# Attention over 128-row tiles: values zero-padded by half, grouped roots, rows added by transfers, combines started on early rows

## The reference

```python
CHUNK = 64; H, DK = 16, 16
q = phi(rope(heads(xn @ Wq + bq)));  k = phi(rope(heads(xn @ Wk + bk)))   # xn = rmsnorm(x); phi = elu + 1
v = heads(xn @ Wv + bv);             g = heads(sigmoid(xn @ Wg + bg))
def step(carry, chunk):                   # chunks of 64 rows, in order
    S = S + k^T v ;  Z = Z + k.sum(rows)  # the chunk's own rows are in the sum
    num = q @ S   ;  den = q @ Z + 1e-6
    return (S, Z), g * (num / den)
x1 = x + out @ Wo + bo
xr = rmsnorm(x1)                          # MoE 1: router softmax, top 2 of 8, 1280 rows per expert at most
x2 = x1 + sum_over_experts(gate * (gelu(xr @ W1) @ W2))
x3 = layernorm(x2)                        # MoE 2: the same with a gated (silu) expert, on layernorm(x3)
out = layernorm(x3 + sum_over_experts(gate * glu(...)))
```

## Time and profile before

| what | us |
|---|---|
| median of three runs (lowest, highest) | 1609.31 (1609.05, 1611.48) |
| the profiled execution | 1607.13 |
| its span | 1605.2 |
| PE busy in the span | 1491.0 (93%) |
| DVE, POOL, ACT busy | 1025.9, 790.6, 729.9 |

### The profile page before, as it was taken

The page is one execution under the profiler, slowest core; times in us unless marked ns, Lnnn a source line. Parts: engine busy times, 40 slices in busy tenths (PEclk is TensorE's granted clock), DMA queues, the critical chain, the costliest instruction groups (busy, mean ns, idle before and its releaser), DMA issues. The chain is left out here.

```text
span 1605.2 us, 36263 instructions
## 1 busy us (share of the span) xinstructions
PE 1491.0 (93%) x11777; PEld 1435.2 (89%) x11777; DVE 1025.9 (64%) x2891; ACT 729.9 (45%) x1737; POOL 790.6 (49%) x799
## 2 busy tenths in 40 slices
PE   5999995799999999999967999999999999999990
PEld 4877774799999999999866999999999999999990
DVE  4888887567667667667374556565655656565553
ACT  3666554445455455555353434344343434343324
POOL 3899981456666566664322443444344344334420
PEclk9999996799999999999976999999999999999995
DMA  7111110333433343352412141323132132312216
GB/s 245 38 37 41 41 41 20 112 95 46 100 92 49 95 96 54 87 128 37 144 80 102 27 115 30 105 33 108 30 75 66 30 105 33 112 27 31 35 15 216
DMA packets 63829, 119.28 MB, mean 74 GB/s; under 512 B 14481, under 2 KB 52881, under 8 KB 61585
## 3 DMA queue, kind: packets, MB, share of 16 engines
q0 software_dynamic: 35840, 42.38, 16.1%
q1 hardware_dynamic: 27920, 76.07, 13.1%
HBM read 79.71 MB, written 38.71 MB: 74 GB/s over the span
## 5 line engine op out<-in xcount | busy, mean ns | idle before, releaser
L841 POOL DMA_INDIRECT acc<-E_ysb,IDX x160 | 258.4, 1615 | 133.8 <-ACT E_ysb L931 65.3
L836 POOL DMA_INDIRECT E_mg<-meta,IDX x160 | 151.0, 944 | 336.1 <-DVE E_gate L952 310.2
L968 DVE TENSOR_TENSOR E_hraw<-E_sg,bank 128x256 f32<-128x256 f32 x320 | 134.6, 421 | 283.3 <-ACT E_sg L904 283.3
L1021 PE MATMUL bank<-E_xT,ws 128*128 128x256 f32 x960 | 271.5, 283 | 5.0 <-DVE E_xT L943 5.0
L1022 PE MATMUL bank<-E_xT,ws 128*128 128x256 f32 x960 | 271.0, 282 | 0.0
L1023 PE MATMUL bank<-E_xT,ws 128*128 128x256 f32 x960 | 270.7, 282 | 0.0
L979 DVE TENSOR_TENSOR E_hT<-E_hraw,E_hT 128x256 fp32r<-128x256 f32 x640 | 259.3, 415 | 0.0
L975 DVE CAST E_hT<-E_hraw 128x256 fp32r<-128x256 f32 x640 | 201.1, 314 | 60.0 <-ACT E_hraw L907 52.9
L904 ACT ACTIVATE E_sg<-bank 128x256 f32<-128x256 f32 x320 | 121.4, 384 | 253.1 <-PE bank L1023 251.4
L1021 PEld LDWEIGHTS bank<-E_xT,ws 128*128 128x128 f32 x960 | 182.5, 190 | 5.8 <-issue 5.8
L1021 PE MATMUL bank<-ws,E_hT 128*128 128x256 f32 x640 | 183.7, 287 | 0.0
(11 more groups left out here) (201 smaller groups left out, 3990.4 us busy)
## 6 DMA issues: line engine op xcount, KB each, us to landing
wraw<-in_w_ffn SPq DMA_DIRECT2D x8, 3072.0 KB, 10.4
wraw<-in_w_moe SPq DMA_DIRECT2D x8, 2048.0 KB, 8.0
X<-acc SPq DMA_DIRECT2D x16, 512.0 KB, 6.8
xn<-A_xn SPq DMA_DIRECT2D x32, 128.0 KB, 1.7
acc<-X SPq DMA_DIRECT2D x32, 128.0 KB, 1.8
acc<-X SPq DMA_DIRECT2D x8, 512.0 KB, 2.6
out<-C_xo SPq DMA_DIRECT2D x8, 512.0 KB, 2.8
X<-in_x SPq DMA_DIRECT2D x3, 1024.0 KB, 11.4
```

The source lines that it names most:

```text
L836: nc.gpsimd.indirect_dma_start(out=mg[:, j, :], out_offset=None, in_=meta_dram, in_offset=at_slots(u, j)).then_inc(s_gm, 16)
L841: nc.gpsimd.indirect_dma_start(out=acc_dram, out_offset=at_slots(u, j), in_=ysb[:, j, :], in_offset=None, compute_op=ALU.add).then_inc(s_y ...
L968: V.tensor_tensor(hraw[:, f % RING, :], sg[:, f % RING, :], bank[f % RING][:, UW:2 * UW], ALU.mult).then_inc(s_hm, 1)
L1021: nc.tensor.matmul(out, wh, mh, start=first, stop=False)
```

## The change

- `add_chunk` reads all 128 partitions of `phi`. Its other operand is `vz`, which holds tile n's values in the 64 rows of chunk c and zeros in the others. DVE writes the values once to `vf`, at the end of the step before, and ACT copies the two halves into `vz` after its `ex`.
- DVE no longer makes `og`. It makes `ng = (tanh + 1) * num` (directly behind `den`), and POOL multiplies by `rden` to give `og`; the 0.5 of the sigmoid goes into Wo, which POOL halves once. ACT's copy `0.5 t + 0.5` is gone. DVE's second mask comes before its rotary product (L437).
- The roots: `r1` for tiles (0), (1 to 3), then four at a time, `r2` for two tiles at a time, so `xn` and the logits' scaling come in pairs, at odd tiles.
- POOL's sum X + x1 is gone. SP stores `x1` to `acc1`, and POOL issues four accumulating transfers of 8 tiles of X into `acc1` (`add_plain`), in steps 11, 19, 27 and in the routing block.
- The end of attention waits for no stores; E1 waits for them. The weight load is cut in two halves, the constants too, the scaling of the weights goes into ACT's copy, the first X rows come as one tile, PE runs 16 fp32 matmuls on zeros at the start, and the folding of the router's weights is moved behind the first tile's work.
- The last scatter of each expert block is not waited for in it. SP loads the first two groups of X when all but the last unit's scatters have landed, the other six in the next block. `keep_busy` goes from 46 to 26 and from 12 to 4.
- All blocks are made with `no_gpsimd_drain=True`.

```diff
+def add_plain(nc, pool, io, X, kept, g):
+    t = slice(g * 8, (g + 1) * 8)
+    for b in range(2):
+        pool.wait_ge(kept[f"x1{b}"], 16 * (g + 1) * 4)
+    nc.gpsimd.dma_start(by_partition(io["acc1"])[:, t, :], X[:, t, :], accum_op=ALU.add).then_inc(kept["plus"], 16)
...
-            sp.wait_ge(s_ac, 16 * NT)
...
                 if (n := at(-1)) is not None:
+                    pool.wait_ge(s_ng, n + 1)
                     pool.wait_ge(s_rden, n + 1)
-                    pool.wait_ge(s_g, n + 1)
-                    after(pool, s_og, n - 1)
-                    nc.gpsimd.tensor_tensor(by_head(gr[:, n % 2, :]), by_head(gt[:, n % 2, :]),
+                    after(pool, s_to, n - 1)
+                    nc.gpsimd.tensor_tensor(by_head(og[:, n % 2, :]), by_head(ng[:, :]),
                                             rden[:, :, :].rearrange("p k h -> p (k h)").unsqueeze(2).to_broadcast([P, H, DK]),
-                                            ALU.mult).then_inc(s_gr, 1)
+                                            ALU.mult).then_inc(s_og, 1)
-                if (n := at(-2)) is not None:
-                    pool.wait_ge(s_xb, n + 1)
-                    pool.wait_ge(s_x1, n + 1)
-                    nc.gpsimd.tensor_tensor(X[:, n, :], X[:, n, :], x1[:, n % 2, 0:D], ALU.add).then_inc(s_xacc, 1)
...
+                if t in (11, 19, 27):
+                    add_plain(nc, pool, io, X, kept, t // 8 - 1)
...
+                    act.wait_ge(s_vf, n + 1)
+                    after(act, s_sa, 2 * n - 2)
+                    for c in range(2):
+                        rows = slice(c * CHUNK, (c + 1) * CHUNK)
+                        nc.scalar.activation(vz[rows, n % 2, c, :, 0:P], vf[rows, :, :], ACT.Copy).then_inc(s_vz, 1)
...
             def add_chunk(n, c):
-                rows = slice(c * CHUNK, (c + 1) * CHUNK)
...
-                    ins = nc.tensor.matmul(s_ps[:, k, :], phi[rows, n % 2, D + k * P:D + (k + 1) * P],
-                                           va[rows, n % 2, k, :], start=False, stop=True, skip_group_check=True)
+                    ins = nc.tensor.matmul(s_ps[:, k, :], phi[:, n % 2, D + k * P:D + (k + 1) * P],
+                                           vz[:, n % 2, c, k, :], start=False, stop=True, skip_group_check=True)
...
+            sp.wait_ge(s_ys, 16 * UT * (UNITS - 1))
+            for g in range(HEAD):
+                t = slice(g * G, (g + 1) * G)
+                sp.dma_start(X[:, t, :], by_partition(acc_dram)[:, t, :]).then_inc(s_head[g], 16)
...
-            pool.wait_ge(s_ys, 16 * UT * UNITS)
...
-                keep_busy(nc, bank[7], ws[0], 46)
+                keep_busy(nc, bank[7], ws[0], 26)
...
-        block = ctx.enter_context(nc.Block())
+        block = ctx.enter_context(nc.Block(no_gpsimd_drain=True))
```

More of the change, by code:

```diff
@@ L36 @@
 UT = UW // P
+G = 4
+GROUPS = NT // G
+HEAD = (UPE - 1) * UW // (G * P)
 SC = E * TILES_E
@@ L93, in after @@
         eng.sem_inc(passed, 1)
-LEAD = 3
+LEAD = 5
 LAG = 2
+R1_GROUPS = [(0, 1), (1, 4)] + [(a, a + 4) for a in range(4, NT, 4)]
+X_SPANS = [(0, 1), (1, 4), (4, 8), (8, 16), (16, 24), (24, 32)]
 WX = 4 * D + E
@@ L219, in _ @@
             sp.dma_start(bo[:, :], io["bo"].partition_broadcast(P)).then_inc(loads, 16)
-            sp.dma_start(bcol[:, :], io["bcol"]).then_inc(loads, 16)
-            for g in range(1, 5):
+            sp.dma_start(cst[:, C_ID + P:C_N], io["consts"][:, C_ID + P:C_N]).then_inc(l_cst, 16)
+            for g in range(2, len(X_SPANS)):
                 rows_in(g)
@@ L304, in _, with high, turned @@
         def _(act):
-            for k in range(KD):
-                act.wait_ge(s_w, 2 * k + 2)
-                nc.scalar.activation(wsp[:, 0, k, :], wqkvg[:, k, :], ACT.Copy).then_inc(s_wh, 1)
+            def high(k, part):
+                nc.scalar.activation(wsp[:, 0, k, part], wqkvg[:, k, part], ACT.Copy, scale=cols[:, k:k + 1]).then_inc(s_wh, 1)
+            def turned(n):
+                act.wait_ge(s_tx, n + 1)
+                after(act, s_pjg, n - 1)
+                after(act, s_xl, n - 1)
+                nc.scalar.activation(xT[:, n % 2, 0, :, :], tx_ps, ACT.Copy).then_inc(s_xT, 1)
+            act.wait_ge(l_cols, 16)
+            act.wait_ge(l_wa, 16)
+            for k in range(KD):
+                high(k, half_a)
+            turned(0)
+            act.wait_ge(l_wb, 32)
+            for k in range(KD):
+                high(k, slice(2 * D, 4 * D))
+            act.wait_ge(s_wrs, KD)
+            for k in range(KD):
+                nc.scalar.activation(wsp[:, 0, k, 4 * D:WX], wrs[:, k, :], ACT.Copy).then_inc(s_wh, 1)
             def step(t, at):
@@ L386, in step @@
             def step(t, at):
+                if t == 0:
+                    dve.wait_ge(l_id, 16)
+                    for m in range(KD):
+                        V.tensor_scalar(bob[:, m, :], ident, 0.0, cols[:, 2 * KD + m:2 * KD + m + 1], ALU.mult, ALU.add).then_inc(s_bob, 1)
+                    dve.wait_ge(l_cst, 16)
                 if (n := at(-1)) is not None:
@@ L450, in _ @@
         def _(pe):
-            pe.wait_ge(early, 16 * 5)
-            pe.wait_ge(s_cst, 4)
+            pe.wait_ge(s_cst, 1)
+            for _ in range(WARM):
+                nc.tensor.matmul(b_to[:, 0:KD * SW], zeros[:, 0:P], zeros[:, :], start=True, stop=True)
             def add_chunk(n, c):
-                rows = slice(c * CHUNK, (c + 1) * CHUNK)
                 if n % TPB == 0 and c == 0:
@@ L495, in step @@
                     after(pe, s_qk, n)
-                    project(n, b_p0[:, :], slice(0, 2 * D)).then_inc(s_pj0, 1)
-                if (n := at(2)) is not None:
-                    loaded(pe, n)
-                    after(pe, s_xl, n)
-                    for k in range(KD):
-                        ins = nc.tensor.transpose(tx_ps[:, k, :], X[:, n, k * P:(k + 1) * P], ident)
-                    ins.then_inc(s_tx, 1)
+                    project(n, b_p0[:, :], half_a).then_inc(s_pj0, 1)
+                if (n := at(2)) is not None and n:
+                    turn(n)
                 if (n := at(0)) is not None:
@@ L846, in free_rows @@
                 pool.wait_ge(s_xgn if glu else s_tg, n * UT if glu else n)
+            if kept:
+                for b in range(2):
+                    pool.wait_ge(kept[f"xn{b}"], 16 * NT // 2)
             x_rows(0)
@@ L1100, in turned @@
             return turn_banks[n % 5][:, 0:D].rearrange("p (k t) -> p k t", k=KD)
-        block = ctx.enter_context(nc.Block())
+        block = ctx.enter_context(nc.Block(no_gpsimd_drain=True))
         @block.sync
         def _(sp):
-            for g in range(GROUPS):
+            sp.wait_ge(s_ys, 16 * UT * UNITS)
+            for g in range(HEAD, GROUPS):
                 t = slice(g * G, (g + 1) * G)
```

292 lines of the change are left out of this document (164 added, 128 removed).

## The result

The changed kernel takes 1588.83 us (median of 4, 1585.68 to 1590.84) against 1610.26 for the kernel before (1609.05 to 1611.48): a ratio of 0.987, 95% interval 0.9849 to 0.9891. Predicted were 1581, with a range from 1565 to 1592. The profiled execution of the changed kernel took 1588.1, its span is 1586.3. Measured again in another set of runs (z_after) it took 1588.89. All but one of the executions in this document had a mean granted clock of 0.95 to 0.96; one of f1_fill21, at 0.625, took 2152.42, and no profile of it exists.

What follows compares the result with a forecast made beforehand. The prediction took PE as full in the expert blocks, with holes at their ends, and a DVE-PE ring as binding attention steps. Its terms, 9.1 + 7.6 + 2.5 + 4.6 + 3.0 = 26.8, gave 1581 us, range 1565 to 1592.

Steps and rivals of the forecast that it cites:

- End of E1: First expert block's end: first transposes at 780.9 instead of 790.00; gain 9.1 us, from 4.8 to 9.7.
- The block ends with POOL's issue: At the first expert block's end: the block ends with POOL's last issue, at 777.6, which is 6.1 us before 783.71.
- End of E2: Second expert block's end: it ends at 1571.2, the third group waits for rows until 1576.9; gain 7.6 us, 3.3 to 9.8.
- second rival: Both expert blocks' ends keep their 4.2 us of silence, 8.5 together, so 1581 becomes 1590; chance 0.11.
- End of attention: Last logits to next block: the switch gives 2.35, the tail's chain changes little; gain 2.5 us, 1.5 to 3.5.
- Start: Kernel's start: half the weights first gives 3.6, moved folding of router weights 1; gain 4.6 us, bounds -1 and +6.5.
- Attention steps: The 29 attention steps: 6.83 us each, from a ring of DVE and PE, against a mean of 6.93; gain 3.0 us.
- first rival: Attention steps: PE was the bound and its drains go, step 6.2 us, 17 us more gained, time 1564; chance 0.2.
- third rival: POOL issues the accumulating transfers row by row, 12.4 us per 8 tiles, 35 us lost, time 1616; chance 0.06.

Runs made afterwards that it cites:

- f1_fill21: Changed kernel with 21 instead of 26 filling matmuls at the end of the first expert block: 1588.67 us, ratio 0.9871 to the kernel before.
- a6_wx_first: Changed kernel with ACT's two copies of the folded router weights ahead of step 0's exponential and value copies: 1588.84 us, ratio 0.9863 to the kernel before.
- c6_more: Changed kernel with og after phi, vf between masks, ACT's copies first, last-tile fillers, 21 fillers ending E1, expert weight slices moved: 1566.37 us, ratio 0.9722.
- a1_drain: Changed kernel with POOL's drain put back at the ends of its five blocks: 1595.66 us, ratio 0.990 to the kernel before.
- a7_tail_fill: Changed kernel with four filling matmuls on zeros before PE's waits in the last tile: 1589.76 us, ratio 0.9874 to the kernel before.
- a2_rows64: Changed kernel with the state update over 64 of the 128 partitions again: 1603.24 us, ratio 0.9944 to the kernel before.
- c1_og_vf: Changed kernel with POOL's og waiting for DVE's next phi and DVE's vf formed between the two masks: 1572.29 us, ratio 0.976 to the kernel before.
- b2_ends_only: Changed kernel with the whole attention block of the kernel before, its drain and waits included: 1593.61 us, ratio 0.9905 to the kernel before.

## Why the prediction was right, and where its steps failed

The time came out 8 us over the forecast and inside the range, since the largest terms were right in the main. By the table the gain is 7.9 short of the sum of 26.8: the attention steps and their tail are 5.3 of it, the end of E1 1.8, and the stretches put at nothing 2.4; the start and the end of E2 gave 1.6 more than was counted.

- **End of E1, 9.1 against 7.3.** The early loads, the missing silence and SP's wait for the landing were right. The step "The block ends with POOL's issue" was not. It put the next block 1.8 after the start of the last scatter's issue; it began 2.7 after, behind PE's 26 fillers, and neither f1_fill21 nor the end of E2 shows POOL's issue holding a block at all. That cost 0.8. And the first groups ran at the lower clock, 0.63 and 0.77 for 0.38 and 0.48; from the first transposes on the stretch took 62.5 instead of 61.6, another 0.9. In a6_wx_first the granted clock was 1.00 there and the stretch took 67.00, a gain of 8.9. With fewer fillers as well (c6_more) it took 65.87, a gain of 10.0, so 9.1 was not the most that was to be had: four fillers at a clock of 1.00 cost 0.25 each there, and not the 0.37 that the sum took from rows 1, where the windows show 0.50 from 787 to 789.
- **End of E2, 7.6 against 8.0.** Right, by its own step: the third group is late. The block's end itself came 3.6 earlier than forecast, before POOL's last issue, which changed nothing, since the rows were what was waited for.
- **The second rival, that block ends don't change**, fell: a1_drain shows 3.99 of silence with the drain at both ends; without it, none is left that POOL causes.
- **End of attention, 2.5 against -0.1.** The step said that the block switch gives 2.35 and the tail's own chain changes little. The switch did fall (from the last logits to routing, 2.62 to 0.80). The chain grew from 12.67 to 14.63: PE's groups are shorter and phi is longer, so PE idled 1.93 before the phi of the last tile (1.12 before), the clock fell from 236 on, and matmul groups took up to 2.1 times as long (the numerators 1.42 for 0.69). a7_tail_fill gave it back. No step of the prediction looked at PE's idle time there. How much it costs is partly chance: in the second profile the chain took 12.91 and the stretch gained 1.6.
- **Start, 4.6 against 5.8, and 3.7 in the second profile of the same kernel.** The first qk stands at 14.44 (17.98 in the earlier trace rows), inside what was asked for. What hung on the clock wasn't counted: ACT's two copies behind ex leave PE idle at 24, and the clock decides over 2 us or more.
- **Attention steps, 3.0 against 0.3.** This is the term that failed. The 6.83 was worked out from a step without the expert's weights (6.84 before, rows 5), but it was set against the mean of 6.93, which holds the sixteen steps with weights. Like against like the forecast was a gain of 0.01 a step, about what came: plain steps went from 6.84 to 6.85. The 0.10 that made the 3.0 was the weights' share, and nothing in the sum takes that away. The kernel before lost some 0.1 in each of the sixteen steps; the change gathered that loss in four dear steps, 0.5 each, with rot now after ra and POOL's weight slice beside it, and no step of the prediction looked there. That 6.83 itself came so near is luck: phi's delay was counted at 0.09 ("up to 0.3") and is 0.42; the waits for PE were counted at 0.75 and are 0.57; DVE's other work came out 0.13 under the 5.99.
- **The first rival (PE was the bound)** had the right floor, 6.2, and the wrong owner: a2_rows64 shows that PE's wider form saves 0.40 a step, the windows that PE sits idle for as much of it (3.5 of 60), and c1_og_vf that PE can run steps of 6.2 to 6.4. It takes both DVE and PE to let go.
- **The third rival** fell: POOL's issue of an accumulating transfer took 0.91 to 1.10, in four cases, where the rival needed 9; the transfers landed after 7.9 to 10.4.

So the 21 us are 15 for the block ends (b2_ends_only shows them alone) and 4 to 6 for the start in the changed kernel's two profiles (only 1.0 in that of f1_fill21, at the lower clock). The new state update freed 0.40 a step on PE, and the new order spent it again on DVE: phi beside og costs 0.42, and 0.56 of waiting between the masks is left unfilled.

## What to carry to other kernels

Before moving an operation of one engine, look at what then runs beside it on the other engine: an og of 0.62 on POOL cost DVE 0.42 each step, and one wait took it away. A wait that an order opens between two uses of PE is room for another operation of the engine that waits; fill it before adding buffers. And where PE runs out of work at the edge of a stage, price the clock of what follows, or give it something idle to do. When a forecast is worked out from one step, compare it with the same kind of step, and not with a mean over several kinds.

## What the runs showed that was not expected

- Without the drain the other engines enter the next block, together, while POOL is still issuing in the last: ACT at 1556.82, DVE at 1556.86, POOL's last issue at 1558.59.
- POOL's root on 128x4 elements beside DVE's rot leaves it at 0.69; a slice of 128x256 beside it makes it 1.20.
- The first expert block, measured as in the table, took between 460.3 and 465.7 over the fourteen profiles, the kernel before and the changed one both at 460.3 to 460.4, and the block with the old attention (b2_ends_only) at 464.3. In the long ones PE waits in the last units, and in c1_og_vf three of POOL's gathers take 2.3 to 2.6 instead of 1.0 and one scatter 3.4 instead of 1.6. It does not go by the attention's order; why it happens stays open. It is as large as the gains of a6_wx_first and a7_tail_fill, which therefore stand in their stretches and not in a median of their own.
